# First convolution's weights and patches loaded in two parts, GpSimd's first patch sum behind the centring, 9 fewer small products

## The chip, the cores and the metric

One core of a Trainium2 chip runs the kernel. The metric is the device time of one execution in microseconds (us). The engines are called by the profile's short names: PE is TensorE (PEld its weight loads), DVE is VectorE, ACT is ScalarE, POOL is GpSimd and SP is SyncE, which here only starts DMA transfers. Each engine runs its own instructions in the order in which they stand, and engines wait for each other through semaphores.

## The reference

A batch of 64 images (3 x 84 x 84) goes through a patch embedding, two attentions over patches, two layers of delta attention with a gated feed-forward, and a feed-forward with blockwise quantized operands. The part that the change touches is the first step and what it feeds:

```python
pe = conv_general_dilated(pixel_values, conv_w, (PS, PS), 'VALID')      # PS = 14, C = 256
grid = pe.reshape(b, C, h, CS, h, CS)
red = grid.mean(axis=(3, 5)).reshape(b, C, hw).transpose(0, 2, 1)
win = grid.transpose(0, 2, 4, 3, 5, 1).reshape(b, hw, N, C)
q = _ln(red, la_ln_q_g, la_ln_q_b) @ la_wq
kv = _ln(win, la_ln_kv_g, la_ln_kv_b) @ la_wkv
```

A patch has 3 x 14 x 14 = 588 numbers, so the convolution is a product of a 588 x 256 weight with the patches. Each layer norm subtracts the mean over the 256 channels.

## The kernel before, in words

The 588 input numbers of a patch are padded to five chunks (KC = 5) of 128 partitions. `cw` holds the weights (128 partitions x 5 x 256, f32), `xg` the patches in six groups g of 384 columns each (128 x 5 x 384 per group); both are views of larger tiles, so the profile calls them `cwb` and `big`. There is no scheduler: every engine's order is as written.

- **SP** starts all loads of the beginning back to back on one queue (lines 242 to 253, then 236 and 238): the weights, patch group 0, patch group 1, the vectors, the first part of the token weights `wt`, patch groups 2 and 3, and so on. Each load adds 16 to a semaphore of its own when it has landed.
- **DVE** centres the weights: `centred(at, end, done)` takes the mean over the 256 channels (line 712), divides it by 256 (line 714) and subtracts it (line 716), first for chunks 0 and 1, then for chunks 2 to 4. Each of its three steps adds 1 to the semaphore `cwc`, so that `cwc` is 3 after the first part and 6 after the second. Line 721 then scales the means for a later use, and DVE goes on to sums over the convolution's output (line 726).
- **PE** first multiplies a tile of ones 35 times by itself with 32 x 64 results that nobody reads (`keep_clock_briefly(7, 35)`, line 1428). Then it waits for `cwc` at 3 and for patch group 0, does the products of chunks 0 and 1 for both halves of the channels (line 1436), waits for `cwc` at 6, and does chunks 2 to 4 of group 0 (`conv(0, 0)` and `conv(0, 1)`, line 1265). Products for the vectors, group 1, more weight products and groups 2 to 5 follow. In the profile each f32 product counts twice, so the 35 products are 70 entries and the four of line 1436 are 8.
- **POOL** sets up the ones (line 272) and then sums the three column blocks of each patch group (`patch_sum(g)`, line 289), groups 0 to 2 first, 8 additions in all. The sums of squares `square_sum` (line 296) come behind them on POOL; PE needs the first three in `stat(0)` (line 1297) and the patch sums themselves in `red_mean(0)` (line 1346).
- **ACT** copies the finished convolution chunks out of PSUM (line 345) and squares them (line 338).

Two pairs of semaphores are of interest. `kqb_mm` is raised once after the products of line 1452 and `vb_mm` once after those of line 1457; likewise `gvb_mm` after line 1486 and `ub_mm` after line 1491.

Of the kernel before, what the change touches and what calls it, by code (L numbers as in the profile page):

```python
# [23 lines left out]
KC, KP = 5, 128  # L24
# [36 lines left out]
def build(nc, xp, cw_d, vec_d, wt_d, wl_d, wf_d, cst_d, out):  # L61
    ctx = ExitStack()
    with ctx:
# [17 lines left out]
        ones = sb("ones", [P, P])  # L81
# [4 lines left out]
        part = sb("part", [P, 2, CH, P])  # L86
        redc = sb("redc", [P, CH, NW])
# [117 lines left out]
        def lw(at, n=C, c=CH):  # L205
# [5 lines left out]
        wd = lw(L_D, C, FC)  # L211


        once = """sqsum cw vecs consts tokw tokw2 ffnw cwc ones conv copied squared xsum part redc redq var_mm rsr
            vec_mm vmean cls_v cls_mm kqb_mm kqb vb_mm vbias wkvg wqg q_mm q k_mm1 k_free stat_mm rk softmax score
            attn v_mm1 vprod vsum acc gath aggT mean_mm redb wcen proj_mm loc gq_mm u gvb_mm gvw ub_mm ub sel sql gst_mm
            gsc_mm gv_mm rsg gsm ga_e attp gpr gag_mm gag gp_mm mod_mm xc x_sq x_var x_rs hx m0_mm m0 h0 wq wq_t wqT
            zeros fin_sq fin_ms fin_rs fin_y h1_t h1 stats rs3 xn xq xq_t xqT gu_mm gate hh hq hq_t hqT
            out_mm outs stored"""
# [19 lines left out]

        @blk_.sync  # L240
        def _(sp):
            sp.dma_start(cw[:, :, :], cw_d).then_inc(S["cw"], 16)
            sp.dma_start(xg[:, 0], xp[0]).then_inc(s_x[0], 16)
            sp.dma_start(xg[:, 1], xp[1]).then_inc(s_x[1], 16)
            sp.dma_start(vec[:, :], vec_d).then_inc(S["vecs"], 16)
            sp.dma_start(wt[:, 0:T_PR], wt_d[:, 0:T_PR]).then_inc(S["tokw"], 16)
            sp.dma_start(xg[:, 2], xp[2]).then_inc(s_x[2], 16)
            sp.dma_start(xg[:, 3], xp[3]).then_inc(s_x[3], 16)
            sp.dma_start(wf[:, :], wf_d).then_inc(S["ffnw"], 16)
            sp.dma_start(xg[:, 4], xp[4]).then_inc(s_x[4], 16)  # L250
            sp.dma_start(xg[:, 5], xp[5]).then_inc(s_x[5], 16)
            sp.dma_start(wt[:, T_PR:NTW], wt_d[:, T_PR:NTW]).then_inc(S["tokw2"], 16)
            sp.dma_start(cst[:, :], cst_d).then_inc(S["consts"], 16)
            load_layer(sp, 0, 0)
            load_layer(sp, 0, 1)
            for l in range(1, LAYERS):
                sp.wait_ge(S["wo_mm"], EACH["wo_mm"] * (l - 1) + 2)
                load_layer(sp, l, 0)
                sp.wait_ge(S["dn_mm"], EACH["dn_mm"] * (l - 1) + 2)
                load_layer(sp, l, 1)  # L260

            o_v = out.rearrange("t s c -> s t c")
            for p in range(3):
                sp.wait_ge(S["outs"], p + 1)
                for a in range(2 if p < 2 else 1):
                    sp.dma_start(o_v[2 * p + a], h1[64 * a:64 * a + 64, p, :]).then_inc(S["stored"], 16)
            sp.wait_ge(S["stored"], 16 * SLOTS)


        @blk_.gpsimd  # L270
        def _(pool):
            nc.gpsimd.memset(ones[:, :], 1.0 / C).then_inc(S["ones"], 1)
            nc.gpsimd.memset(h1[:, 2, :], 0.0).then_inc(S["zeros"], 1)

            n = [0]

            def patch_sum(g):

                pool.wait_ge(s_x[g], 16)
                hf = g // 3  # L280
                for a in range(3):
                    new = xg[:, g, :, a * P:(a + 1) * P]
                    first = g % 3 == 0 and a == 1
                    if g % 3 == 0 and a == 0:
                        continue
                    old = xg[:, g, :, 0:P] if first else xs[:, hf]
                    if not first:
                        pool.wait_ge(S["xsum"], n[0])
                    nc.gpsimd.tensor_tensor(xs[:, hf], old, new, ALU.add).then_inc(S["xsum"], 1)  # L289
                    n[0] += 1  # L290

            def square_sum(g):

                pool.wait_ge(S["squared"], 2 * g + 2)
                cols = slice(g % 3 * GRP, (g % 3 + 1) * GRP)
                nc.gpsimd.tensor_tensor(sq[:, 0, cols], sq[:, 0, cols], sq[:, 1, cols], ALU.add  # L296
                                        ).then_inc(S["sqsum"], 1)

            def value_sum(un):

                hf, uu = divmod(un, 5)
                pool.wait_ge(S["vsum"], un + 1)
                old = vsum[:, (un - 1) % 3, :] if uu == 1 else vtot[:, hf, :]
                if uu > 1:
                    pool.wait_ge(S["acc"], 4 * hf + uu)
                nc.gpsimd.tensor_tensor(vtot[:, hf, :], old, vsum[:, un % 3, :], ALU.add
                                        ).then_inc(S["acc"], 2 if uu == 1 else 1)

            for g in range(3):
                patch_sum(g)  # L310
            for g in range(6):
                square_sum(g)
            for un in range(1, 4):
                value_sum(un)
            for g in range(3, 6):
                patch_sum(g)
            for un in range(6, 9):
                value_sum(un)

            pool.wait_ge(S["gag_mm"], 1)  # L320
            nc.gpsimd.memset(act[0:64, FC - 1, :], 0.0).then_inc(S["zeros"], 1)
# [309 lines left out]
        def _(dve):  # L631
# [85 lines left out]
                                ALU.subtract).then_inc(S["cwc"], 1)  # L717

            centred(0, 2, 0)
            centred(2, KC, 3)  # L720
            v.tensor_scalar(cmean9[:, :], cmean[:, :], 1.0 / NP_, None, ALU.mult).then_inc(S["cwc"], 1)

# [132 lines left out]
                step(v.tensor_tensor(clsv[:, 12:13], vmean[:, 0:1], vmean[:, 2:3], ALU.add))  # L855

            def key_weights():
                dve.wait_ge(S["kqb_mm"], 1)
                dve.wait_ge(S["vb_mm"], 1)
                v.tensor_copy(vbias[:, 0:CH], ps[:, 4, 10:12]).then_inc(S["vbias"], 1)  # L860
                for c in range(CH):
                    v.tensor_scalar(wkv[:, c, :], wkv[:, c, :], vec[:, V_LKG + c:V_LKG + c + 1], None, ALU.mult
# [23 lines left out]
            def class_values():  # L886
                dve.wait_ge(S["gvb_mm"], 1)
                for c in range(CH):
                    v.tensor_scalar(gwkv[:, c, C:2 * C], gwkv[:, c, C:2 * C], vec[:, V_GKG + c:V_GKG + c + 1], None,
                                    ALU.mult).then_inc(S["gvw"], 1)  # L890
                dve.wait_ge(S["ub_mm"], 1)
                v.tensor_copy(ub[:, :], ps[:, 6, 0:H]).then_inc(S["ub"], 1)

            for c in range(CH):
# [354 lines left out]
        def _(pe):  # L1249
# [178 lines left out]
                    mm(ps[0:32, bank, 0:64], ones[:, 0:32], ones[:, 0:64], start=True, stop=True)  # L1428

            pe.wait_ge(S["ones"], 1)  # L1430
            keep_clock_briefly(7, 35)
            pe.wait_ge(S["cwc"], 3)
            pe.wait_ge(s_x[0], 16)
            for c in range(CH):
                for k in range(2):
                    mm(ps[:, c, 0:GRP], cwc[:, k, c * P:(c + 1) * P], xg[:, 0, k, :], start=(k == 0), stop=False)
            pe.wait_ge(S["cwc"], 6)
            conv(0, 0)
            conv(0, 1)
            pe.wait_ge(S["ones"], 1)  # L1440
# [14 lines left out]
            for j in range(CH):  # L1455
                for c in range(CH):
                    last = mm(ps[:, 4, 10 + j:11 + j], wkv[:, c, C + j * P:C + (j + 1) * P],
                              vec[:, V_LKB + c:V_LKB + c + 1], start=(c == 0), stop=(c == CH - 1))
            last.then_inc(S["vb_mm"], 1)
            conv(2, 0)  # L1460
            conv(2, 1)
            conv(3, 0)
# [27 lines left out]
            for c in range(CH):  # L1490
                last = mm(ps[:, 6, 0:H], vec[:, V_GKB + c:V_GKB + c + 1].broadcast_to([P, P]), u[:, c, :],
                          start=(c == 0), stop=(c == CH - 1))
            last.then_inc(S["ub_mm"], 1)
            conv(5, 0)
            keys(4)
            conv(5, 1)
# [464 lines left out]
```

## Time and profile before

| | us |
|---|---|
| median of 3 runs | 296.84 |
| lowest and highest of the 3 runs | 293.67 and 297.17 |
| span of the profiled execution, first to last instruction | 292.3 |
| the profiled execution's own device time | not recorded beside the three runs |
| PE busy (products), share of the span | 268.0, 92% |
| DVE busy | 206.8, 71% |
| ACT busy | 94.1, 32% |
| POOL busy | 38.0, 13% |

The span is that of one execution and lies 1.4 us below the lowest of the three runs and 4.5 us below their median. Busy shares are averages over a program with very different parts: in the first 85 us PE is nearly always at work, in the delta attention (about 120 to 150 us and 190 to 220 us) PE and DVE take turns on small tiles, and the last 30 us are led by DVE.

### The profile page before, as it was taken

How to read it: one execution, taken by the hardware profiler on the slowest of the kernel's cores; microseconds unless marked ns; L12 is line 12 of the kernel's file. 1: busy time of each engine (PE TensorE's matmuls, PEld its weight loads, DVE VectorE, ACT ScalarE, POOL GpSimd, SP SyncE). 2: the span in 40 equal slices, each digit the busy share in tenths (PEclk: the TensorE clock that was granted, in tenths of full speed). 3: DMA queues.
4: the chain of work that ended last, by engine and by line, in shares of the span. 5: the costliest groups of instructions: out<-in, count | busy, mean ns of one | idle time of the engine just before them, and what ended most of it. 6: DMA issues, size and time to landing. Idle time of an engine off the chain costs nothing.

```text
span 292.3 us, 9910 instructions
## 1 busy us (share of the span) xinstructions
PE 268.0 (92%) x4473; PEld 205.7 (70%) x4473; DVE 206.8 (71%) x413; ACT 94.1 (32%) x235; POOL 38.0 (13%) x35
## 2 busy tenths in 40 slices
PE   8999999999999899968979999978898999789865
PEld 8666678778997778857857766758876676655443
DVE  3649869987689676467686579675667665498992
ACT  1122301330000026656224432665424343351310
POOL 1991100203893100000000000000000000000000
PEclk9999999999999999999966999997985999999999
DMA  7999900000000000000000302500000000000001
GB/s 287 419 422 419 440 32 0 0 0 2 0 0 2 0 1 3 2 4 0 2 4 13 135 0 75 231 4 2 1 4 2 0 2 0 0 1 2 0 0 45
DMA packets 2730, 18.71 MB, mean 64 GB/s; under 512 B 464, under 2 KB 784, under 8 KB 1936
## 3 DMA queue, kind: packets, MB, share of 16 engines
q1 hardware_dynamic: 2704, 18.34, 15.8%
q8 instruction: 20, 0.33, 0.4%
q14 instruction: 6, 0.05, 0.1%
HBM read 18.01 MB, written 0.33 MB: 63 GB/s over the span
## 4 chain that ended last, share of the span: by engine, by line
PE 74%; DVE 18%; ACT 3%; issue 2%; DMA 2%; SPq 0%; DVEq 0%
PE ps L1265 13%; PE ps L1587 8%; PE ps L1309 5%; PE ps L1799 4%; PE ps L1323 4%; PE ps L1568 3%; PE ps L1688 3%; PE ps L1697 3%; PE ps L1719 2%; DMA big<-in_patches 2%; DVE big L1112 2%; DVE wt L1109 2%; PE ps L1255 2%; PE ps L1771 2%; PE ps L1841 2%
## 5 line engine op out<-in xcount | busy, mean ns | idle before, releaser
L1265 PE MATMUL ps<-big,cwb 128*128 128x384 f32 x112 | 37.9, 489 | 0.0
L1265 PEld LDWEIGHTS ps<-big,cwb 128*128 128x128 f32 x112 | 20.9, 190 | 13.0 <-DVE cwb L716 0.3
L1587 PE MATMUL ps<-xT,wl 128*128 128x320 f32 x88 | 24.5, 434 | 0.7 <-ACT wguT L369 0.5
L289 POOL TENSOR_TENSOR xs<-xs,big 128x640 f32<-128x640 f32 x14 | 23.3, 1667 | 1.4
L1587 PEld LDWEIGHTS ps<-xT,wl 128*128 128x128 f32 x88 | 16.6, 190 | 7.8 <-ACT wguT L369 0.7
L1688 PE MATMUL ps<-wt,big 32*32 32x32 f32 x1280 | 14.8, 199 | 5.7 <-DVE wt L1066 2.8
L345 ACT COPY pecT<-ps 128x384 f32<-128x384 f32 x12 | 5.8, 480 | 40.8 <-PE ps L1265 40.8
L1688 PEld LDWEIGHTS ps<-wt,big 32*32 32x32 f32 x1280 | 13.1, 110 | 8.0 <-DVE big L1112 4.0
L1323 PE MATMUL ps<-wt,pecT 128*128 128x256 f32 x72 | 16.5, 380 | 0.6 <-DVE big L821 0.6
L1309 PE MATMUL ps<-wt,pecT 128*128 128x256 f32 x72 | 16.9, 381 | 0.0
L1109 DVE COPY_PREDICATED wt<-cst,ps 128x320 f32<-128x320 int32 x16 | 8.0, 498 | 10.9 <-PE ps L1697 10.9
L1323 PEld LDWEIGHTS ps<-wt,pecT 128*128 128x128 f32 x72 | 13.5, 190 | 3.0 <-DVE big L821 1.0
L1309 PEld LDWEIGHTS ps<-wt,pecT 128*128 128x128 f32 x72 | 13.4, 190 | 2.3
L1697 PE MATMUL ps<-wt,big 32*32 32x32 f32 x1280 | 13.3, 196 | 0.7 <-issue 0.7
L1799 PE MATMUL ps<-big,wl 128*128 128x320 f32 x48 | 13.3, 434 | 0.0
L1697 PEld LDWEIGHTS ps<-wt,big 32*32 32x32 f32 x1280 | 12.5, 106 | 0.9 <-issue 0.9
L726 DVE TENSOR_REDUCE part<-pecT 128x128 f32<-128x384 f32 x12 | 7.1, 594 | 8.4 <-ACT pecT L345 8.3
L1170 DVE TENSOR_TENSOR cwb<-ps,cwb 128x320 f32<-128x320 f32 (+1 forms) x12 | 5.9, 490 | 9.9 <-PE ps L1587 5.7
L1799 PEld LDWEIGHTS ps<-big,wl 128*128 128x128 f32 x48 | 8.8, 190 | 4.2 <-DVE big L1162 1.0
L499 ACT COPY wt<-ps 128x320 f32<-128x320 f32 x16 | 6.8, 426 | 14.4 <-PE ps L1688 14.4
L296 POOL TENSOR_TENSOR sq<-sq 128x384 f32<-128x384 f32 x6 | 6.2, 1044 | 39.9 <-ACT sq L338 39.9
L1841 PE MATMUL ps<-wguT,pecT 128*128 128x352 f32 x32 | 10.0, 466 | 0.9 <-ACT pecT L592 0.9
(306 smaller groups left out, 535.8 us busy)
## 6 DMA issues: line engine op xcount, KB each, us to landing
big<-in_patches SPq DMA_DIRECT2D x6, 960.0 KB, 11.8
wl<-in_layers SPq DMA_DIRECT2D x2, 2176.0 KB, 19.8
wf<-in_ffn SPq DMA_DIRECT2D x1, 2112.0 KB, 17.9
wl<-in_layers SPq DMA_DIRECT2D x2, 1040.0 KB, 15.9
wt<-in_tok SPq DMA_DIRECT2D x1, 1536.0 KB, 24.8
wt<-in_tok SPq DMA_DIRECT2D x1, 768.0 KB, 8.5
cwb<-in_conv SPq DMA_DIRECT2D x1, 640.0 KB, 3.9
cst<-in_constants SPq DMA_DIRECT2D x1, 320.0 KB, 25.0
```

The source lines that it names most:

```text
L289: nc.gpsimd.tensor_tensor(xs[:, hf], old, new, ALU.add).then_inc(S["xsum"], 1)
L726: step(v.tensor_reduce(part[:, min(g % 3, 1), c, :], pecT[:, c, g * GRP:(g + 1) * GRP].rearrange("p (t n) -> p n t", t=3), AX.X, ALU.add))
L1109: v.copy_predicated(tc_[:, g, :], m.unsqueeze(1).broadcast_to([P, NB, 32]), bank32(6 + b, slice(0, P))).then_inc(S["tp"], 1)
L1265: last = mm(ps[:, i % 4, 0:GRP], cwc[:, k, c * P:(c + 1) * P], xg[:, g, k, :], start=(k == 0), stop=(k == KC - 1))
L1309: last = mm(ps[:, 4 + un % 2, t * C:(t + 1) * C], pecT[:, c, i * P:(i + 1) * P], wkv[:, c, 0:C], start=(c == 0), stop=(c == CH - 1))
L1323: last = mm(ps[:, un % 3, t * C:(t + 1) * C], pecT[:, c, i * P:(i + 1) * P], wkv[:, c, C:2 * C], start=(c == 0), stop=(c == CH - 1))
L1568: last = mm(ps[:, bank, cols], lw(at)[:, c, j * P:(j + 1) * P], src[:, c, cols], start=(c == 0), stop=(c == CH - 1))
L1587: last = mm(ps[:, bank, 0:NT], w(c, j), x[:, c, :], start=(c == 0), stop=(c == CH - 1))
L1688: last = mm(ps[r, 4 + b, 32 * k:32 * k + 32], apm[r, NB * b + k, own], tc_[r, NB * b + k, :], start=True, stop=True)
L1697: last = mm(ps[r, 6 + b, 32 * k:32 * k + 32], ttc[r, NB * b + k, :], yc[r, NB * b + k, :], start=True, stop=True)
L1799: last = mm(ps[:, 6 + j, 0:NT], wd[:, i, j * P:(j + 1) * P], act[:, i, :], start=(i == 0), stop=(i == FC - 1))
L1841: last = mm(ps[:, b + w, 0:352], xqT[:, c, P * p:P * p + P], wguT[:, c, 352 * w:352 * w + 352], start=(c == 0), stop=(c == CH - 1))
```

## The change

On SP the load of the weights becomes two, chunks 0 and 1 and chunks 2 to 4, and so does that of patch group 0; the four go out in the order weights 0-1, patches 0-1, weights 2-4, patches 2-4. Two semaphores, `cw_rest` and `x0_rest`, stand for the second parts: DVE waits for `cw_rest` before the second part of the centring, PE for `x0_rest` before `conv(0, 0)`. POOL's first patch sum waits for `x0_rest` and for `cwc` at 6 as well. The small products of ones on PE are 26 instead of 35. The semaphores `vb_mm` and `ub_mm` are gone: the same instructions raise `kqb_mm` and `gvb_mm` a second time, and the waits ask for 2.

```diff
-            sp.dma_start(cw[:, :, :], cw_d).then_inc(S["cw"], 16)
-            sp.dma_start(xg[:, 0], xp[0]).then_inc(s_x[0], 16)
+            sp.dma_start(cw[:, 0:2, :], cw_d[:, 0:2, :]).then_inc(S["cw"], 16)
+            sp.dma_start(xg[:, 0, 0:2, :], xp[0, :, 0:2, :]).then_inc(s_x[0], 16)
+            sp.dma_start(cw[:, 2:KC, :], cw_d[:, 2:KC, :]).then_inc(S["cw_rest"], 16)
+            sp.dma_start(xg[:, 0, 2:KC, :], xp[0, :, 2:KC, :]).then_inc(S["x0_rest"], 16)
             sp.dma_start(xg[:, 1], xp[1]).then_inc(s_x[1], 16)
@@
                 pool.wait_ge(s_x[g], 16)
+                if g == 0:
+                    pool.wait_ge(S["x0_rest"], 16)
+                    pool.wait_ge(S["cwc"], 6)
@@
             centred(0, 2, 0)
+            dve.wait_ge(S["cw_rest"], 16)
             centred(2, KC, 3)
@@
             def key_weights():
-                dve.wait_ge(S["kqb_mm"], 1)
-                dve.wait_ge(S["vb_mm"], 1)
+                dve.wait_ge(S["kqb_mm"], 2)
@@
-                dve.wait_ge(S["ub_mm"], 1)
+                dve.wait_ge(S["gvb_mm"], 2)
@@
             pe.wait_ge(S["ones"], 1)
-            keep_clock_briefly(7, 35)
+            keep_clock_briefly(7, 26)
             pe.wait_ge(S["cwc"], 3)
             pe.wait_ge(s_x[0], 16)
             ...
             pe.wait_ge(S["cwc"], 6)
+            pe.wait_ge(S["x0_rest"], 16)
             conv(0, 0)
             conv(0, 1)
@@
-            last.then_inc(S["vb_mm"], 1)
+            last.then_inc(S["kqb_mm"], 1)
@@
-            last.then_inc(S["ub_mm"], 1)
+            last.then_inc(S["gvb_mm"], 1)
```

SP's queue at the start of the program, before and after; `cwb` is the weights' tile, `big` the patches', and the numbers are partitions by f32 elements:

```order
L242 DMA cwb<-in_conv 128x1280
L243 DMA big<-in_patches 128x1920
L244 DMA big<-in_patches 128x1920
L245 DMA vec<-in_vectors 128x36
L246 DMA wt<-in_tok 128x1536
```

```order
L242 DMA cwb<-in_conv 128x512
L243 DMA big<-in_patches 128x768
L244 DMA cwb<-in_conv 128x768
L245 DMA big<-in_patches 128x1152
L246 DMA big<-in_patches 128x1920
```

Patch group 1, third in the queue before, is fifth now, and the bytes ahead of it are the same.

PE at the start of the program, before and after; each row names the tile written and the tiles read, the shape, and the semaphores that it waits for:

```order
L1428 MATMUL ps<-ones 32x64 [waits s_ones]
L1428 MATMUL ps<-ones 32x64 x34
L1436 MATMUL ps<-big,cwb 128x384 [waits s_patches0,s_cwc]
L1436 MATMUL ps<-big,cwb 128x384 x3
L1265 MATMUL ps<-big,cwb 128x384 [waits s_patches0,s_cwc]
L1265 MATMUL ps<-big,cwb 128x384 x5
```

```order
L1433 MATMUL ps<-ones 32x64 [waits s_ones]
L1433 MATMUL ps<-ones 32x64 x25
L1441 MATMUL ps<-big,cwb 128x384 [waits s_patches0,s_cwc]
L1441 MATMUL ps<-big,cwb 128x384 x3
L1270 MATMUL ps<-big,cwb 128x384 [waits s_patches0,s_x0_rest,s_cwc]
L1270 MATMUL ps<-big,cwb 128x384 x5
```

Nothing changes place on PE; nine small products are gone, and the row of chunks 2 to 4 waits for one thing more.

## Rows read from the trace of the kernel before

**Rows 1.** the page: the span, and the chain that ended last by engine

```profile
span 292.3 us, 9910 instructions
...
PE 74%; DVE 18%; ACT 3%; issue 2%; DMA 2%; SPq 0%; DVEq 0%
```

**Rows 2.** the chain that ended last: start us, us, what

```profile
7.14 2.82 PE ps L1436 x8
...
14.16 3.33 PE ps L1265 x10
...
45.54 1.90 PE ps L1297 x18
...
82.84 1.85 PE ps L1309 x8
84.78 0.70 DVE prod L763
```

**Rows 3.** windows, PE alone: window, us, PE busy (x entries), granted clock, DMA share, GB/s

```profile
10.00:40.00 30.00, 30.00 (x115) 1.00 0.92 384
40.00:84.50 44.50, 44.50 (x229) 1.00 0.00 1
```

**Rows 4.** timeline of PE: start us, us, instruction, [idle before <-releaser]

```profile
0.99 5.89 PE L1428 MATMUL ps<-ones 128*32 128x64 f32 x70 [0.99 <-POOL ones L272]
7.14 2.82 PE L1436 MATMUL ps<-big,cwb 128*128 128x384 f32 x8 [0.25 <-DMA big<-in_patches]
```

**Rows 5.** timeline of SP: when each DMA is issued, and for how long

```profile
0.74 0.38 SPq L242 DMA_DIRECT2D cwb<-in_conv  x1
1.18 0.42 SPq L243 DMA_DIRECT2D big<-in_patches  x1
1.64 0.43 SPq L244 DMA_DIRECT2D big<-in_patches  x1
```

**Rows 6.** issue to landing, lines 242, 243 and 244 in this order

```profile
DMA to landing us min/median/max: 3.9/3.9/3.9
...
DMA to landing us min/median/max: 5.8/5.8/5.8
...
DMA to landing us min/median/max: 7.8/7.8/7.8
```

**Rows 7.** DMA issues by line: KB each, median us from issue to landing

```profile
out<-h SPq DMA_DIRECT2D x5, 64.0 KB, 2.0
```

**Rows 8.** timeline of DVE: the centring of the weights

```profile
4.68 0.69 DVE L712 TENSOR_REDUCE cmean<-cwb 128x2 f32<-128x512 f32 x1 [4.68 <-DMA cwb<-in_conv]
5.40 0.17 DVE L714 TENSOR_SCALAR cmean<-cmean 128x2 f32<-128x2 f32 x1
5.61 0.69 DVE L716 TENSOR_TENSOR cwb<-cwb,cmean 128x512 f32<-128x512 f32 x1
6.21 0.95 DVE L712 TENSOR_REDUCE cmean<-cwb 128x3 f32<-128x768 f32 x1
7.20 1.44 DVE L714 TENSOR_SCALAR cmean<-cmean 128x3 f32<-128x3 f32 x1
8.67 0.96 DVE L716 TENSOR_TENSOR cwb<-cwb,cmean 128x768 f32<-128x768 f32 x1
```

**Rows 9.** windows, PE alone, over the small products of ones

```profile
0.98:4.78 3.80, 3.79 (x36) 1.00 0.77 274
4.78:6.72 1.94, 1.94 (x37) 1.00 1.01 420
```

**Rows 10.** timeline of POOL: the 8 patch sums of groups 0 to 2

```profile
7.07 1.54 POOL L289 TENSOR_TENSOR xs<-big 128x640 f32<-128x640 f32 x1 [5.88 <-DMA big<-in_patches]
8.69 12.16 POOL L289 TENSOR_TENSOR xs<-xs,big 128x640 f32<-128x640 f32 x7
```

**Rows 11.** windows, PE alone, two later stretches

```profile
148.20:158.30 10.10, 8.76 (x136) 0.50 0.01 2
...
216.50:226.60 10.10, 8.64 (x174) 0.50 0.01 3
```

More of the change, by code:

```diff
@@ L211, in build @@
         wd = lw(L_D, C, FC)
-        once = """sqsum cw vecs consts tokw tokw2 ffnw cwc ones conv copied squared xsum part redc redq var_mm rsr
-            vec_mm vmean cls_v cls_mm kqb_mm kqb vb_mm vbias wkvg wqg q_mm q k_mm1 k_free stat_mm rk softmax score
-            attn v_mm1 vprod vsum acc gath aggT mean_mm redb wcen proj_mm loc gq_mm u gvb_mm gvw ub_mm ub sel sql gst_mm
+        once = """sqsum cw cw_rest x0_rest vecs consts tokw tokw2 ffnw cwc ones conv copied squared xsum part redc redq var_mm rsr
+            vec_mm vmean cls_v cls_mm kqb_mm kqb vbias wkvg wqg q_mm q k_mm1 k_free stat_mm rk softmax score
+            attn v_mm1 vprod vsum acc gath aggT mean_mm redb wcen proj_mm loc gq_mm u gvb_mm gvw ub sel sql gst_mm
             gsc_mm gv_mm rsg gsm ga_e attp gpr gag_mm gag gp_mm mod_mm xc x_sq x_var x_rs hx m0_mm m0 h0 wq wq_t wqT
```

## Prediction

> **What bounds the kernel now.** I read the page first: the span of the profiled execution is 292.3 us, and 74% of the chain that ended last is PE [rows 1]. The chain itself tells where a change at the start of the program counts. It runs through PE from 7.14 us, when the first real product starts, to 84.8 us, where DVE takes over [rows 2], and the windows show PE busy in all of 10 to 84.5 us [rows 3]. So for the first 85 us PE works down its list without a pause. An earlier start of that list moves everything up to there by as much, if no load and no other engine gets in the way. Behind 84.8 us each step waits for the one before it, so the lead should be kept to the end.
>
> What sets the start at 7.14 us? On PE the small products of ones begin at 0.99 us and are through at some 6.8 us; then PE is idle 0.25 us for patch group 0 [rows 4]. Group 0 is issued at 1.18 us [rows 5] and lands 5.8 us later [rows 6], at 6.98 us. The centring of chunks 0 and 1 on DVE is through at 5.61 + 0.69 = 6.30 us [rows 8]. So three things meet before the first product: ones, centring, patches, and the patches are last.
>
> **The loads.** Weights land at 0.74 + 3.9 = 4.64 us, group 0 at 6.98, group 1 at 1.64 + 7.8 = 9.44 [rows 5, 6]. A group is 128 x 1920 x 4 bytes = 960 KB, and two of them took 2.34 and 2.46 us, so the queue moves some 410 KB per us. The 640 KB of weights then account for 1.56 us of the time before 4.64, and 3.08 us is where the stream effectively starts. In the new order 256 KB of weights land at 3.08 + 0.62 = 3.70 us, 384 KB of patches at 4.64, 384 KB of weights at 5.58, and the last 576 KB at 6.98. SP needs 0.44 to 0.46 us from one issue to the next [rows 5], so the fourth load goes out at about 2.1 us and group 1 at about 2.5 instead of 1.64. It was in flight for 7.8 us, nearly all of it queueing, so 0.9 us of later issue does not move its landing at 9.44. PE reaches it at 14.16 us before [rows 2] and would at 12.7 now, 3.3 us after the landing. The loads behind it go out 0.9 us later too, and are covered in the same way.
>
> The split is the unknown of this change: no row shows a 256 KB load at the head of the queue. The bounds are from below the stores of 64 KB, 2.0 us from issue to landing [rows 7], which with the 192 KB more at 410 KB per us give 0.74 + 2.0 + 0.47 = 3.2 us; and from above the landing of the whole weights, 4.64 us. I take 3.70, by the two landings of the same queue.
>
> The Trainium skill, page "DMA: Bandwidth & Descriptors", section "Anatomy of one DMA", gives a load a fixed cost of about 2.0 us and its bytes at 436 GB/s on top; by that, an estimate from the page, the first weights would land at 0.74 + 2.0 + 0.6 = 3.3 us. That lies near my lower bound, and as the next parts show it would change nothing, since another term comes last.
>
> **The centring.** The first part takes from 4.68 to 6.30 us, 1.62 us [rows 8]. From 3.74 it ends at 5.36 us. The second part has no wait before; now it waits for weights 2-4 at 5.58 us. It took from 6.21 to 9.63 us, 3.42 us, of which the small step of line 714 is 1.44, against 0.17 for its twin on chunks 0 and 1 [rows 8]. That step runs from 7.20 to 8.64 us, and POOL's first patch sum from 7.07 to 8.61 [rows 10]: DVE's step ends as POOL's does, 0.03 us later. With POOL's sum behind `cwc` at 6 the 1.27 us go. The second part then takes 2.15 us, from 5.62 to 7.77. If the stall had another cause and stayed, it would end at 9.04.
>
> **The small products.** They set the start now. The first 36 entries take 3.79 us, 105 ns each, the other 34 take 1.94 us, 57 ns each [rows 9]. The granted clock reads 1.00 in both windows, but the pace nearly doubles, so PE went from the lower of its two levels (1.2 GHz) to the higher (2.4 GHz) at about 4.78 us, after 3.8 us of unbroken small products. 26 products are 52 entries: 36 until 4.78 us, and 16 x 57 ns = 0.91 us, which ends at 5.69. The centring (5.36) and patches 0-1 (4.64) are ready before. The first real product starts at about 5.7 us instead of 7.14, which is a gain of **1.4 us**. PE goes over from the ones to the real products without a pause, where it paused for 0.25 us before, so I expect no fall of the clock.
>
> Here the Trainium skill has a rule against the change: page "TensorE: Matmul & The Clock Gate", Part 1, says that the rise of the clock is bought with a time of sustained work and not with a number of products, and comes at another moment in every run. It is the clock rival below.
>
> **Chunks 2 to 4.** The 8 entries of line 1436 take 2.82 us [rows 4], so PE asks for the rest at 5.7 + 2.8 = 8.5 us. The second centring is there at 7.77, 0.7 us ahead, and patches 2-4 at 6.98, 1.5 us ahead: the new wait on PE costs nothing. Were the stall on DVE still there, PE would wait about 0.5 us. Before, this step was ready at 9.63 and PE at 9.96, so it is no gain by itself: POOL's delay only keeps the earlier start from being lost here.
>
> **What is delayed.** POOL's 8 patch sums now start at about 7.8 us instead of 7.07. They take until 8.69 + 12.16 = 20.85 us [rows 10] and would end at about 21.6. Queued behind them are the sums of squares, for which PE waits at 45.5 us [rows 2], 44.1 when moved up: over 20 us of cover. POOL's overlap moves from line 714 to the step of line 721 and to DVE's later small steps, which it slowed before as well; DVE's first sum of the convolution waits for ACT anyway. Price 0, at most some tenths on DVE that PE, which alone is on the chain there [rows 2], does not feel.
>
> **The semaphores.** The merged pairs are raised by the same PE instructions in the same order, and each reader waits for the value that the later one gives. Price 0; one wait fewer on DVE.
>
> **Sum.** 292.3 - 1.4 = 290.9 us of span. The profiled span lies 4.5 us below the median of the three runs, and I take that distance as it is: 296.84 - 1.4 = **295.4 us**, 0.5% faster.
>
> **Rivals.**
>
> 1. *The first part doesn't land earlier (the split doesn't do what it says).* If weights 0-1 land at 4.64 us, the centring ends at 6.3 and PE starts at 6.35: gain 0.8 us, 296.0. Landings between give between 0.8 and 1.4. For it: no row has a short load at the head of the queue. Against it: the queue has a steady pace over three loads. If the four shorter loads also slow the stream, it is about even, 296.8.
>
> 2. *A half-speed stretch of PE falls elsewhere.* The profile has two stretches of 10 us at a granted clock of 0.50 (the 1.2 GHz level), 148.2 to 158.3 and 216.5 to 226.6, with PE busy for 8.76 and 8.64 us in them [rows 11]. Work bound by PE takes twice as long there, so one is worth up to 4.4 us, and as part of it is waiting I put it at 3. They begin in or behind the small-tile work of the attention, which moves by 1.4 us. One fewer gives about 292.4, one more 298.4. The three runs before, 3.5 us apart, look like just that. It happens with and without the change, so it widens the range more than it moves the time.
>
> 3. *The clock rises late, and the kernel gets slower.* The place is PE between 5.7 and 10 us. With 52 entries all at the low level the ones end at 0.99 + 52 x 0.105 = 6.45 us, and the real products then run at half pace until the clock rises. The cost against the forecast is 0.75 us for the later end and half of the time from 6.45 to the rise. It turns into a loss when the rise comes later than about 7.8 us, against 4.78 in the profile; a rise at 10 us gives 0.75 + 1.8 = 2.55, so 298.0 us. For it: fewer ones are left as a reserve. Against it: the real products follow at once and keep PE busy, and a late rise made the 70 entries of before later too.
>
> 4. *The gain is lost at another wait within the first 85 us.* That needs an engine or load that lags PE by less than 1.4 us now. The chain shows only PE there, so I give it little: 296.8.
>
> **How the numbers follow.** Forecast (1.0 to 1.6 us gained): 0.60, 295.4. Rival 1: 0.13, 296.0 to 296.8. Rival 2: one stretch fewer 0.08, 292.4; one more 0.09, 298.4. Rival 3: 0.04, 298.0. Rival 4: 0.06, 296.8. The median of three runs of before is itself one draw from 293.7 to 297.2, which enters each case. The range 292.2 to 298.2 holds the forecast with rivals 1, 3 and 4 and about half of each side of rival 2. Faster by over 2% would be below 290.9 us, slower by over 2% above 302.8; 2% is about what a measurement of this kernel can tell from no change. No case reaches either; I leave 0.03 and 0.01.
>
> **What would show it.** In the profile after: the first load lands at about 3.7 us after the span's start, DVE's first reduction starts then and line 719 (714 before) takes 0.17 us both times; the small products end at about 5.7 and the first real product follows at once; POOL starts at about 7.8; `conv(0, 0)` has no wait; each later product of PE up to 83 us starts 1.4 us earlier. I am wrong if the first real product starts after 6.4 us, if PE waits before chunks 2 to 4, or if the lead seen at 10 us is gone by 85.

## The result and the profile after

The changed kernel takes 298.05 us (median of 14 runs, 295.12 to 299.53), the kernel before 296.63 (median of 14, 293.67 to 298.77). The ratio is 1.0078, with a 95% interval of 1.0049 to 1.0107: slower by 0.8%, where I had forecast 0.5% faster. All ratios here leave out executions over 1.5% above the fastest of their kernel, here three of the kernel before (298.19 to 298.77) and none of the changed one; over all executions the means are 1.5 us, 0.5%, apart. The profiled execution has a span of 296.9 us, 4.6 more than that of before [rows 1]:

```profile
span 296.9 us, 9876 instructions
...
PE 76%; DVE 16%; issue 3%; ACT 2%; DMA 2%; SPq 0%; DVEq 0%
```

In the chain that ended last, "issue" (the engine waits for nothing that the profile shows) has gone from 2% to 3%, and PE from 74% to 76%.

**The start.** PE's timeline of the changed kernel (start, us, instruction, idle before) answers to [rows 4]:

```profile
0.99 5.40 PE L1433 MATMUL ps<-ones 128*32 128x64 f32 x52 [0.99 <-POOL ones L274]
6.33 2.85 PE L1441 MATMUL ps<-big,cwb 128*128 128x384 f32 x8
9.53 4.14 PE L1270 MATMUL ps<-big,cwb 128*128 128x384 f32 x12 [0.36 <-DVE cwb L721]
...
33.30 0.60 PE L1281 MATMUL ps<-ones,redq 128*128 128x1 f32 x4
```

The first real product starts at 6.33 us instead of 7.14, the products of chunks 2 to 4 at 9.53, where the timeline of the kernel before has:

```profile
9.79 4.03 PE L1265 MATMUL ps<-big,cwb 128*128 128x384 f32 x12
```

In the changed kernel they waited for DVE's centring. DVE's timeline, against [rows 8]:

```profile
3.58 0.69 DVE L717 TENSOR_REDUCE cmean<-cwb 128x2 f32<-128x512 f32 x1 [3.58 <-DMA cwb<-in_conv]
...
7.33 0.95 DVE L717 TENSOR_REDUCE cmean<-cwb 128x3 f32<-128x768 f32 x1 [2.14 <-DMA cwb<-in_conv]
8.32 0.17 DVE L719 TENSOR_SCALAR cmean<-cmean 128x3 f32<-128x3 f32 x1
8.52 0.96 DVE L721 TENSOR_TENSOR cwb<-cwb,cmean 128x768 f32<-128x768 f32 x1
...
31.67 1.12 DVE L742 SCALAR_TENSOR_TENSOR redc<-part 128x256 f32<-128x256 f32 x1
```

The stall of line 714 is gone: 0.17 us at 8.32, where it was 1.44. But the second centring starts at 7.33 us, because it waited for weights 2-4. From issue to landing, lines 242 to 245 (weights 0-1, patches 0-1, weights 2-4, patches 2-4), against [rows 6]:

```profile
DMA to landing us min/median/max: 2.8/2.8/2.8
...
DMA to landing us min/median/max: 3.4/3.4/3.4
...
DMA to landing us min/median/max: 5.7/5.7/5.7
...
DMA to landing us min/median/max: 6.6/6.6/6.6
```

Issued at 0.74, 1.18, 1.64 and 2.12 us, the four land at 3.5, 4.6, 7.3 and 8.7. The first two come as forecast (3.70, 4.64), the other two 1.7 us later than forecast (5.58, 6.98).

The last rows of the two timelines show where even the small lead ends. DVE's `redc` step, 0.42 us before, takes 1.12 us at 31.67, while a sum of squares of POOL runs from 31.51 to 32.50 us. ACT's square and PE's line 1281 come behind it, and PE is then 0.1 us behind the old kernel instead of 0.15 ahead.

**The loops.** So the start is even, and the 4.6 us come later. The list of PE's waits without a visible cause (line, total, times, longest), before:

```profile
PE ps L1697 <- issue: 0.7, 2, 0.4
...
PE ps L1712 <- issue: 0.5, 2, 0.2
...
PE ps L1734 <- issue: 0.2, 1, 0.2
```

and after:

```profile
PE ps L1703 <- issue: 3.7, 2, 2.3
...
PE ps L1740 <- issue: 1.2, 2, 1.0
...
PE ps L1718 <- issue: 0.5, 2, 0.2
```

That is 1.4 us before and 5.4 after. They lie in and just behind the two loops over small 32 x 32 products (lines 1688 and 1697 of before, in a hardware loop of four rounds with 320 entries and as many weight loads each, once in each attention layer). PE's timeline there, before:

```profile
125.83 0.89 PE L1688 MATMUL ps<-wt,big 32*32 32x32 f32 x80
128.11 0.89 PE L1688 MATMUL ps<-wt,big 32*32 32x32 f32 x80 [1.40 <-DVE wt L1066]
128.85 0.58 PE L1697 MATMUL ps<-wt,big 32*32 32x32 f32 x45
129.72 1.20 PE L1697 MATMUL ps<-wt,big 32*32 32x32 f32 x115 [0.29 <-issue]
...
142.32 1.31 PE L1712 MATMUL ps<-pecT,cst 128*128 128x320 f32 x4 [0.24 <-issue]
...
198.79 1.59 PE L1697 MATMUL ps<-wt,big 32*32 32x32 f32 x124 [0.40 <-issue]
```

and after:

```profile
126.94 0.89 PE L1694 MATMUL ps<-wt,big 32*32 32x32 f32 x80
128.43 0.89 PE L1694 MATMUL ps<-wt,big 32*32 32x32 f32 x80 [0.59 <-DVE wt L1071]
129.16 0.73 PE L1703 MATMUL ps<-wt,big 32*32 32x32 f32 x63
132.23 1.54 PE L1703 MATMUL ps<-wt,big 32*32 32x32 f32 x97 [2.34 <-issue]
...
145.19 1.31 PE L1718 MATMUL ps<-pecT,cst 128*128 128x320 f32 x4 [0.24 <-issue]
...
150.25 0.25 PE L1740 MATMUL ps<-wt,big 32*32 32x32 f32 x4 [1.01 <-issue]
...
202.67 1.12 PE L1703 MATMUL ps<-wt,big 32*32 32x32 f32 x106 [1.32 <-issue]
```

In the old kernel the first half of a round is 80 entries, then 80 that wait for DVE (1.40 us), then come 45 of the 160 entries of the second half; PE pauses 0.29 us and goes on. In the new one PE comes 63 entries far and pauses 2.34 us. 63 is 45 + 18, and 18 entries are the 9 small products that were taken out at the start of the program. The pause stands at a fixed distance in the instruction stream from the start, not at a fixed place in the code.

The longer pauses, 4.0 us more in sum, do not simply add up to 4.0 of the 4.6 us. PE is 0.26 us ahead of the old kernel at 122 us, 1.1 behind at the start of the first loop (126.94 against 125.83), 2.9 behind after it (line 1718 against 1712), 3.7 at the start of the second loop, 3.2 after that one and 4.6 at the end. The 1.4 us between 122 and the first loop fall in a stretch in which the granted clock reads 0.51, where the old kernel's reads 1.00:

```profile
121.90:125.30 3.40, 3.40 (x70) 0.51 0.02 5
```

Of the lateness at the first loop 0.8 us are made good, since the wait for DVE is shorter by that much (0.59 instead of 1.40 us); the pause of 2.34 us comes on top. So this one profile mixes two things, the pauses and the clock; run b26 below shows the first of them without a difference ahead of the loop.

What PE seems to wait for is in the transfers of the instruction queue, which the page gives as 20 packets of 0.33 MB in both kernels, 16 KB each. One of them starts in 127.4 to 128.1 us before and none between 126.0 and 127.4:

```profile
q8 instruction: 1, 0.02, 8.6%
```

In the changed kernel there is none from 126.0 to 129.4 us; it starts after that, in 129.4 to 131 us:

```profile
q8 instruction: 1, 0.02, 5.4%
```

By the trace's transfer records the starts are 127.48 and 129.47 us. PE's pause ends 2.2 us after the first (129.72) and 2.8 after the second (132.23). In the old kernel the block was under way while PE waited for DVE anyway; in the new one its transfer started only 1.0 us behind that wait, in the middle of dense products. In all 17 profiles this pause ends 2.2 to 2.8 us after such a transfer starts; that PE waits for its own instructions is read from this and from the place that moves with them.

The Trainium skill, page "Runtime: NRT & Kernel Launch", section "Instruction fetch mechanics", describes this as PE's instruction memory being refilled in blocks of 16 KiB by the sequencer's own queue, mostly hidden, except that a taken branch to a target outside the two blocks at hand forces a fetch first. The 16 KB agree with the trace's packets; that the cost is mostly hidden holds here only for some placements.

### The profile page after: what moved, and what is told of

Read it like the earlier page. It is cut to its first block, busy times and chain, and to the rows that moved or that the text cites. A ratio compares the mean times of both kernels' runs of the same rounds, so it can differ in the third digit from the quotient of the medians.

```text
span 296.9 us, 9876 instructions
## 1 busy us (share of the span) xinstructions
PE 270.7 (91%) x4455; PEld 206.9 (70%) x4455; DVE 205.4 (69%) x413; ACT 94.0 (32%) x235; POOL 37.1 (13%) x35
## 4 chain that ended last, share of the span: by engine, by line
PE 76%; DVE 16%; issue 3%; ACT 2%; DMA 2%; SPq 0%; DVEq 0%
PE ps L1270 12%; PE ps L1593 8%; PE ps L1314 5%; PE ps L1805 4%; PE ps L1328 4%; PE ps L1847 3%; PE ps L1574 3%; PE ps L1694 3%; PE ps L1703 3%; PE ps L1428 3%; DVE big L1117 2%; DMA cwb<-in_conv 2%; DVE wt L1114 2%; PE ps L1260 2%; PE ps L1771 2%
## 5 line engine op out<-in xcount | busy, mean ns | idle before, releaser
L294 POOL TENSOR_TENSOR xs<-xs,big 128x640 f32<-128x640 f32 x14 | 22.5, 1610 | 1.4
```

## The experiments

Two theories stood at first. P: the number of PE instructions ahead of the loops decides where an instruction block ends in them, and the 9 products taken out moved it badly. L: the split loads cost the time. All ratios are to the kernel before, and "pauses" is the sum of PE's waits on "issue" in the run's profile, as above.

### One part at a time

```diff
 # a35: the changed kernel
-            keep_clock_briefly(7, 26)
+            keep_clock_briefly(7, 35)
 # b26: the kernel before
-            keep_clock_briefly(7, 35)
+            keep_clock_briefly(7, 26)
 # split35: as a35
-                    pool.wait_ge(S["cwc"], 6)
 # pool35: the kernel before
                 pool.wait_ge(s_x[g], 16)
+                if g == 0:
+                    pool.wait_ge(S["cwc"], 6)
```

> The changed kernel with 35 small products instead of 26. Theory P (placement of PE's instructions): the loss comes from PE's pauses without a visible cause in the two loops of small-tile products (5.4 us in the profile of the changed kernel, 1.4 us in that of before), and these depend on how many PE instructions stand ahead of the loops; with 35 they fall back to under 2.5 us and the ratio to before is 0.997 to 1.003. Theory L (the split loads cost the time): weights 2-4 still land at about 7.3 us, and the ratio stays at 1.005 to 1.010.

> The kernel before with 26 small products and nothing else changed. Theory P: PE's unexplained pauses rise to 4 to 6 us and the ratio to before is 1.005 to 1.011, though the first real product starts at 7.1 us as before. Theory L: nothing that matters is changed, ratio 0.998 to 1.002.

> The changed kernel with 35 small products and POOL's first patch sum waiting only for its patches. Theory P: ratio 0.997 to 1.003, unexplained pauses under 2.5 us. Theory L: 1.005 to 1.012. POOL starts at about 8.7 us, when patches 2-4 land, and slows the centring of weights 2-4 by up to 1.3 us, so the first conv(0) product of chunks 2 to 4 starts later than in the changed kernel's 9.5 us.

> The kernel before with only POOL's first patch sum behind the centring (cwc at 6). Theory P: ratio 0.998 to 1.003; line 714's second execution takes 0.17 us instead of 1.44, the centring is through at 8.4 instead of 9.6 us, and PE, which asked at 9.8, gains nothing. Theory L: the same. A third theory, D (POOL's later sums slow DVE's small steps at 22 to 33 us): PE waits about 0.3 us before line 1276 and the ratio is 1.001 to 1.003.

| run | ratio to before, 95% interval | pauses, us |
|---|---|---|
| a35 | 1.0007 (0.9972 to 1.0042) | 2.3 |
| b26 | 1.0104 (1.0050 to 1.0158) | 3.9 |
| split35 | 0.9981 (0.9947 to 1.0015) | 4.0 |
| pool35 | 1.0001 (0.9966 to 1.0037) | 1.3 |

b26 has nothing of the change but the 9 products, whose end PE did not even wait for, and it is 1% slower. a35 has all of the change but those, and is even. That is theory P and against L. PE's timeline of b26, first half of a round and the pauses:

```profile
128.93 0.73 PE L1697 MATMUL ps<-wt,big 32*32 32x32 f32 x63
131.57 1.54 PE L1697 MATMUL ps<-wt,big 32*32 32x32 f32 x97 [1.92 <-issue]
...
145.08 1.31 PE L1712 MATMUL ps<-pecT,cst 128*128 128x320 f32 x4 [0.24 <-issue]
...
202.11 1.65 PE L1697 MATMUL ps<-wt,big 32*32 32x32 f32 x106 [0.75 <-issue]
```

63 entries and a pause of 1.92 us, at the same place as in the changed kernel, with the loads of before. Up to the first loop this profile is a constant 0.07 us behind that of the kernel before; after the loop it is 2.8 us behind (145.08 against 142.32), and 2.6 at the end. Practically the whole loss arises in that one loop.

The pause itself grew by only 1.6 us of these 2.7 (1.92 instead of 0.29). Soon after it begins, from 130.3 us on, the granted clock reads 0.50 for 6.8 us, and in the same window of the kernel before 1.00 (b26 first, then before):

```profile
130.30:137.10 6.80, 5.40 (x385) 0.50 0.01 2
130.30:137.10 6.80, 5.75 (x587) 1.00 0.01 2
```

All seven profiles with 22, 26, 28, 39 or 44 products' worth of instructions ahead of the first loop have such a stretch of 3.4 to 6.9 us somewhere from 130 to 140 us, and so has split35's; the nine others, all with 31, 32 or 35, have none. So the block's place costs time in two ways, by the pause and by a stretch at the lower clock level that comes with it: 1.6 us and, as the difference, an estimated 1.1 us in b26. In all of them the pause begins before the clock falls. No run has one without the other, so how much of a ratio belongs to which stays open.

The 4.0 us of pauses of split35 are from an execution of 298.04 us, its slowest; the other eleven took 293.32 to 296.62 us. The expectation of under 2.5 us was not met in it; the ratio came as expected.

pool35 shows that POOL's delay does remove the stall (line 714 took 0.17 us and the centring was through at 8.4 us) and brings nothing by itself. In its profile the clock rose only at 6.9 us and the first real product started at 7.82, so the earlier centring could not show there. Theory D, that POOL's later sums cost time on PE, was not seen there; it is seen in the profiles of the changed kernel, a35 and afterpad, where POOL starts at 9.3 us or later: `redc` takes 1.12 to 1.13 us in these three and 0.42 to 0.43 in all others, and PE loses 0.25 us at line 1281.

### Elsewhere, and other counts

```diff
 # afterpad: the changed kernel (26 at the start), at about 102 us
             keep_clock(0, 1, 192)
+            for _ in range(9):
+                mm(ps[0:32, 0, 0:8], ones[:, 0:32], ones[:, 0:8], start=True, stop=True)
 # b31, b22, b44: the kernel before
-            keep_clock_briefly(7, 35)
+            keep_clock_briefly(7, 31)   # 22, 44
```

> The changed kernel (26 small products at the start) with 9 tiny products of ones (32 x 8 results that nobody reads) added far later, at about 102 us, where PE waits 0.7 us for DVE anyway. Theory P says that only the number of PE instructions ahead of the loops counts: the pauses without a visible cause fall under 2.5 us and the ratio to before is 0.996 to 1.002. Theory W (the 9 products are missed at the start, as warm-up of the clock): the pauses stay at 4 to 6 us and the ratio at 1.005 to 1.010.

> The kernel before with 31 small products (4 fewer). Theory P: the time is a step or a saw-tooth in the number of instructions, so this lies either with 35 (ratio 0.998 to 1.002, pauses under 2.5 us) or with 26 (1.005 to 1.012, pauses of 3 us or more), not between them. A theory in which each missing product costs its share gives 1.004 to 1.005.

> The kernel before with 22 small products (13 fewer). Theory P: as bad as 26 or back to the level of 35, by its pauses (3 us or more: 1.005 to 1.012; under 2.5 us: 0.998 to 1.002). A theory in which each missing product costs its share gives 1.014.

> The kernel before with 44 small products (9 more). They end at about 7.2 to 7.8 us, so the first real product starts up to 0.6 us later. Theory P: pauses anywhere between 0 and 6 us, and the ratio follows them: 1.000 to 1.003 with pauses under 2.5 us, 1.007 or more with 4 us. A theory in which each product saves its share gives 0.991 to 0.993.

afterpad is the decisive run: it gives back the 9 products' instructions, but not at the start. Ratio 0.9978 (0.9934 to 1.0023), pauses 1.1 us. The pause is back at 45 entries and short:

```profile
129.90 0.58 PE L1705 MATMUL ps<-wt,big 32*32 32x32 f32 x45
130.71 1.20 PE L1705 MATMUL ps<-wt,big 32*32 32x32 f32 x115 [0.23 <-issue]
...
199.73 1.57 PE L1705 MATMUL ps<-wt,big 32*32 32x32 f32 x124 [0.38 <-issue]
```

Theory W (the products are missed as warm-up) expected 1.005 to 1.010 and falls. The counts:

| small products (kernel before) | ratio, 95% interval | pauses, us |
|---|---|---|
| 22 | 1.0176 (1.0111 to 1.0240) | 5.6 |
| 26 | 1.0104 (1.0050 to 1.0158) | 3.9 |
| 28 | 1.0088 (1.0047 to 1.0130) | 3.1 |
| 31 | 0.9974 (0.9926 to 1.0022) | 1.2 |
| 35 | 1 | 1.4 |
| 39 | 1.0084 (1.0040 to 1.0128) | 6.2 |
| 44 | 1.0197 (1.0139 to 1.0256) | 8.7 |

More products than 35 cost as much as fewer than 31. A part of that is the start, which the small products themselves now hold up: chunks 2 to 4 start at 10.76 us with 39 and at 11.45 with 44 instead of 9.79, in profiles in which the clock rose at 6.5 and 6.8 us. The rest goes with the pauses (the 6.2 us of 39 are from an execution of 302.67 us, where the median is 298.16). With 44 the pauses are others: PE stops a second time near the end of the first round, for the next block, and again in the second layer:

```profile
131.77 1.30 PE L1697 MATMUL ps<-wt,big 32*32 32x32 f32 x128 [0.85 <-issue]
135.77 0.25 PE L1697 MATMUL ps<-wt,big 32*32 32x32 f32 x5 [2.70 <-issue]
...
206.10 1.30 PE L1697 MATMUL ps<-wt,big 32*32 32x32 f32 x128 [2.04 <-issue]
209.55 0.43 PE L1697 MATMUL ps<-wt,big 32*32 32x32 f32 x14 [2.15 <-issue]
```

Between its two pauses in the first round stand 128 entries and as many weight loads, 256 instructions. If one 16 KB transfer brings just these, an instruction has 64 bytes; the 9 products taken out, 18 entries and 18 weight loads, are then 2.3 KB of a block.

In b22 about 1.7 us of the loss is something else. The 22 products end 2.01 us before the first real product starts, which waits for the patches, and 0.4 us after that start the granted clock falls from 1.00 to 0.50 (the 1.2 GHz level) for 3.4 us (window, us, PE busy, granted clock):

```profile
5.30:7.20 1.90, 0.09 (x1) 1.00 1.05 428
7.50:10.90 3.40, 3.40 (x7) 0.50 1.01 406
10.90:14.00 3.10, 3.10 (x10) 1.00 1.02 426
```

The 8 entries of chunks 0 and 1 take 4.51 us there instead of 2.82. In b26's profile the gap was 1.70 us and the clock stayed at 1.00 until 130 us, where the pause is, so b26's loss is not this.

### Between the loops

```diff
 # b26mid: as b26, and in layer 1, ahead of its loop
-                    keep_clock(0, 2, 512)
+                    keep_clock(0, 1, 512)
+                    for _ in range(10):
+                        mm(ps[0:32, 0, 0:8], ones[:, 0:32], ones[:, 0:8], start=True, stop=True)
```

> The kernel before with 26 small products at the start and, between the two loops of small-tile products (at about 181 us, in place of one 512-column filler product), 10 tiny products of ones, so that the second loop has as many PE instructions ahead of it as in the kernel before and the first has 36 fewer. Theory P (placement): around the first loop the pauses are those of 26 products (1.3 to 2.5 us, and 0.3 to 1.0 us some 18 us later), around the second those of before (0.2 to 0.9 us); ratio between the two, 1.003 to 1.008. A theory in which something at the start of the program slows both loops keeps both, ratio 1.008 to 1.012.

Ratio 1.0113 (1.0047 to 1.0179), above the 1.003 to 1.008 that I expected for the total. The places of the pauses came as expected:

```profile
132.62 1.54 PE L1699 MATMUL ps<-wt,big 32*32 32x32 f32 x97 [2.11 <-issue]
...
151.22 0.25 PE L1736 MATMUL ps<-wt,big 32*32 32x32 f32 x4 [0.93 <-issue]
...
203.43 1.79 PE L1699 MATMUL ps<-wt,big 32*32 32x32 f32 x124 [0.52 <-issue]
```

Around the first loop they are those of b26 (97 entries left behind the pause, 2.11 us, and 0.93 us later); in the second layer the pause lies at the place of before (124 entries left) and takes 0.52 us, with none in line 1736. Since b26's own second loop cost only 0.75 + 0.22 us in its profile, only some 0.5 us was there to be saved, too little for the intervals to show. That the total did not fall stays unexplained; in its profile the clock is at the lower level from 121.7 to 125.1 and from 132.0 to 138.8 us, in b26's only in the second place.

### The loads

```diff
 # split31: as split35
-            keep_clock_briefly(7, 35)
+            keep_clock_briefly(7, 31)
 # wfirst31: the changed kernel, 31 products (line not shown)
             sp.dma_start(cw[:, 0:2, :], cw_d[:, 0:2, :]).then_inc(S["cw"], 16)
+            sp.dma_start(cw[:, 2:KC, :], cw_d[:, 2:KC, :]).then_inc(S["cw_rest"], 16)
             sp.dma_start(xg[:, 0, 0:2, :], xp[0, :, 0:2, :]).then_inc(s_x[0], 16)
-            sp.dma_start(cw[:, 2:KC, :], cw_d[:, 2:KC, :]).then_inc(S["cw_rest"], 16)
 # xsplit31: the changed kernel, 31 products (line not shown), weights whole
-            sp.dma_start(cw[:, 0:2, :], cw_d[:, 0:2, :]).then_inc(S["cw"], 16)
+            sp.dma_start(cw[:, :, :], cw_d).then_inc(S["cw"], 16)
             sp.dma_start(xg[:, 0, 0:2, :], xp[0, :, 0:2, :]).then_inc(s_x[0], 16)
-            sp.dma_start(cw[:, 2:KC, :], cw_d[:, 2:KC, :]).then_inc(S["cw_rest"], 16)
@@
-            dve.wait_ge(S["cw_rest"], 16)
```

> The changed loads with 31 small products and POOL's first sum waiting for its patches alone. Theory P: pauses under 2.5 us. The start: ones end at 6.2 to 6.5 us, weights 2-4 land at 6.5 to 7.7 us as in the three runs that had these loads, so the products of chunks 2 to 4 start at 9.0 to 9.9 us against 9.79 before; ratio 0.994 to 1.000. If the load order cost nothing (my forecast's 5.58 us for weights 2-4), they would start at 8.9 us.

> As the changed kernel with 31 small products, and the second part of the weights issued ahead of the first part of the patches. If shorter loads as such slow the stream (theory S), patches 0-1 land at 6 to 7 us instead of 5.6 and the first real product starts at 6.3 to 7.0; weights 2-4 land at 4.7 to 5.5 us and the second centring is through by 7.8. If only the place in the queue matters, weights 2-4 land at 4.6 us and patches 0-1 at 5.6. Chunks 2 to 4 start at 9.0 to 9.6 us, ratio 0.993 to 0.999.

> As the changed kernel with 31 small products, but the weights loaded whole and only patch group 0 in two parts. Weights land at 4.7 us, centring of chunks 0 and 1 through at 6.3, patches 0-1 at 5.6 to 6.2: first real product at 6.4 us, second centring through at 8.5 without POOL's stall, chunks 2 to 4 at 9.1 us against 9.79 before. Theory S: patches 2-4 land at 7.5 to 8.5 us instead of 7.0, which still costs nothing. Ratio 0.993 to 0.999.

| run | landings in the order of issue, us | chunks 2 to 4 start, us | ratio |
|---|---|---|---|
| changed kernel | 3.5, 4.6, 7.3, 8.7 | 9.53 | 1.0078 (1.0049 to 1.0107) |
| split31 | 3.5, 4.5, 6.6, 8.1 | 8.96 | 0.9974 (0.9938 to 1.0011) |
| wfirst31 | 3.5, 4.6, 6.1, 8.7 | 9.07 | 0.9977 (0.9935 to 1.0018) |
| xsplit31 | 4.6, 5.7, 7.2 | 9.78 | 0.9992 (0.9953 to 1.0031) |

These loads have the same bytes in all versions, and before the last of them landed at 6.98 us. In three parts it lands 0.2 us later, in four 1.1 to 1.7 us in this table and 2.1 in a35. Patch group 1 behind them lands at 9.7 us (xsplit31), 10.5 (split31) and 11.1 to 11.2 (wfirst31, the changed kernel) instead of 9.44. So the place of one load in the queue is not what costs: in both orders of four the last lands late. Theory S puts it down to the number of short loads. xsplit31 fits that, but it also leaves the weights whole, so whether the number counts or the cut in the weights' load is not shown. In xsplit31 the weights were in time, but the clock rose only at 6.3 us, the 31 small products ended at about 7.0, and the first real product started at 7.09. For wfirst31 the second centring is through at 7.2 us, so its chunks 2 to 4 follow without a wait:

```profile
6.38 2.85 PE L1441 MATMUL ps<-big,cwb 128*128 128x384 f32 x8
9.07 4.03 PE L1270 MATMUL ps<-big,cwb 128*128 128x384 f32 x12
```

That is the forecast mechanism at work: 9.07 instead of 9.79 us, 0.7 us of lead. split31 has 0.8 us of lead at 81 us and 1.2 us at 110, and then loses all of it in one stretch (0.2 us behind at 126 us):

```profile
120.60:124.00 3.40, 3.40 (x83) 0.51 0.02 5
```

With the granted clock at 0.51 (nearly all of it at the 1.2 GHz level), the 80 entries of line 1664 take 2.37 us instead of 1.56 and those of line 1677 1.83 instead of 1.13. In the old kernel the same work ran at 1.00. The wait for DVE in the loop is then shorter here, so the second 80 products start 0.3 us ahead again. The two profiles differ in where the clock falls, and the profiles of wfirst31, split35, b26mid and the changed kernel have a fall between 120 and 122 us too. Whether an earlier start makes that fall likelier is not settled by one profile each.

### The steps, and the forecast start on its own

> The kernel before with 28 small products (28 fewer PE instruction entries than with 35). The time was level at 31 and 35 and some 1% up at 26. Theory P with one step where an instruction block's border passes a wait: either level (0.995 to 1.002, pauses under 2.5 us) or up (1.005 to 1.012, pauses over 3 us). A gradual loss would give 1.003 to 1.006.

> The kernel before with 39 small products (16 more entries than with 35). 44 gave 1.020. Level (0.996 to 1.003, a little later start by 0.2 us) if the second step lies between 39 and 44, or up by 1% or more with pauses over 4 us if it lies below 39.

b28 is at 1.0088 and b39 at 1.0084 (table above). Both are up, so the level stretch is narrow: 31 and 35 in, 28 and 39 out. By these ratios it is a step between 28 and 31 and not a slope: the intervals of 28 and 31 do not meet. The pause says the same (1.87 us in the first loop with 28, 0.47 with 31). The ratio of 28 alone would be weak evidence: the means over all executions, 297.68 us for b28 and 297.02 for the kernel before, are only 0.7 us apart.

> All weights ahead of the patches as in the run of that order with 31, but 26 small products at the start and 6 tiny ones at 102 us, so that 32 products' worth of instructions stand ahead of the loops. Weights 2-4 land at 5 us, patches 0-1 at 6.2, the first real product starts at 6.2 us or, if the clock rises late, when the ones end; chunks 2 to 4 at 8.9 us without a wait. Theory P: pauses under 2.5 us. Ratio to before 0.993 to 0.999. If the lead is lost again at a half-speed stretch of PE's clock around 120 us, 0.997 to 1.000.

Edit: wfirst31 with 26 small products at the start and 6 of the tiny ones at 102 us. Ratio 0.9994 (0.9944 to 1.0045), pauses 2.7 us, a little over the 2.5 that theory P allowed. The patches landed at 6.84 us, so the first real product started at 6.93 us and chunks 2 to 4 at 9.58: no earlier than with 31. No version is shown to be faster than the kernel before: the best four (b31, split31, wfirst31, afterpad) lie at 0.9974 to 0.9978, each with an interval that reaches over 1.

## Why the prediction was wrong

The measured 298.05 us lie inside my range of 292.2 to 298.2, but that is luck: the range was wide for other reasons, and none of its cases has instruction blocks in it.

- **"The first real product starts at about 5.7 us" (small products).** It was 6.33. The clock rose at 5.9 us in this execution and not at 4.78, so 46 entries of the small products ran at the slow pace. This is my rival 3 in a small size, worth 0.6 us. I had taken the moment of one execution for a property of the kernel; over the 17 profiles the rise comes at 4.0 to 6.9 us. The rule of the Trainium skill that I cited there (page "TensorE: Matmul & The Clock Gate", Part 1), that a count of products does not buy the rise, agrees with this.
- **The loads.** First part right (3.5 and 4.6 us). Weights 2-4 at 7.3 instead of 5.58: the pace of 410 KB per us, read from long loads, does not hold for four shorter ones in the first 9 us. Rival 1 had this in its last sentence ("If the four shorter loads also slow the stream, it is about even, 296.8"), at a small chance; a35, with the same loads and all 35 products, is even (1.0007). That PE would ask at 8.5 us and find the second centring done since 7.77 failed by this (it was done at 9.48), and the start's gain shrank from 1.4 to 0.26 us. The estimate from the Trainium skill's page "DMA: Bandwidth & Descriptors" (section "Anatomy of one DMA"), 3.3 us for the first landing, was 0.2 us short of the 3.5; the page gives its figures for transfers issued by GpSimd, and these are SP's.
- **The stall of line 714.** Right in cause and size: it is gone in all runs where POOL waits for the centring, and present (1.39 to 1.43 us) in b22, b26, b26mid, b28, b31, b39 and b44, where nothing about POOL is changed. pool35, with that one edit, shows the cause. In split35 and split31 POOL waits for patches 2-4 alone and starts late enough; the small step behind the centring takes 1.5 us there, as in the kernel before.
- **What is delayed ("Price 0").** Nearly. POOL started at 9.66 us and not at 7.8, its patch sums ended at 22.6, and its third sum of squares ran beside DVE's `redc`; PE lost 0.25 us there.
- **"Nothing changes place on PE; nine small products are gone": the step that failed.** So says the section on the change, and the prediction follows it: I priced the products by their own time, and the sum has no term for what their absence does to the rest of PE's list; I put it at nothing without a reason. The instructions do not change order, but all that follow stand 36 instructions (18 entries and 18 weight loads) earlier in the stream, and in the first loop the pause is 2.34 us instead of 0.29. Cost alone: b26, 1.0104; taken back: a35, 1.0007, and afterpad, 0.9978. The 1.4 us of "issue" was in the trace of before, in the list of PE's waits, and I passed over it as small.
- **Rival 2 (another half-speed stretch).** It came too: the profile of the changed kernel has the clock at the lower level for some 31 us between its start and 290 us, that of the kernel before for some 24. I took such stretches for chance, equal with and without the change. The one from 132.2 to 135.6 us is one of those that come with the long pause. The mean granted clock of the 14 executions is 0.937 to 0.954, and no execution with 22, 26 or 28 products' worth of instructions ahead of the loops (44 with these 14) is above that; of the 97 of the kernel before that ran beside the experiments, 53 read 0.957 or more.
- **"The lead should be kept to the end".** Not testable on the changed kernel, which had none. In split31 the 0.8 us of lead at 9 us were 1.2 at 110 and 0.3 at 128.

The wrong sign comes from the step that failed, since a35 and afterpad, which differ from the changed kernel only in these instructions, are even; the first two points explain why no gain stood against it.

## What to carry to other kernels

Taking out or adding instructions ahead of a dense stretch or a loop can move where its instruction blocks end, and here that was worth 1%. Before calling such an edit free, look for PE waits on "issue", and compare with a variant that has the same number of instructions and puts the fillers where the engine waits anyway (as afterpad did); a difference of 1% between two counts is no verdict on what the instructions do.

When a load is cut in parts, cost the case that the later parts land late (here by 1.7 us) and leave slack for the wait behind them. And take the moment of the clock's rise from several executions, not from one.

## What the runs showed of the hardware

- The pause in the first loop stood at 27, 37, 45, 53, 59, 63 and 71 of 160 entries for 44, 39, 35, 31, 28, 26 and 22 small products, two entries per product, and at the same place in every variant with that number of products ahead of the loop, wherever they stood (51 for the 32 of wfirstpad).
- It ended 2.2 to 2.8 us after the start of a 16 KB transfer on the instruction queue. With 31 to 44 products that transfer started while PE waited for DVE between the first two groups of 80 entries, or just as that wait ended; with 22 to 28 it started only 1.0 to 1.4 us after the end of the wait. Why it isn't asked for earlier stays open; placing the loop itself on a block's border wasn't tried.
- In eight profiles (the changed kernel, b22, b26, b26mid, b28, b39, b44 and split35) the granted clock read 0.50 or 0.51 for 3.4 to 6.9 us in or behind the pauses of the first loop, which are 1.09 to 2.70 us at their longest there. In the nine others, with 0.23 to 1.15 us, it read 1.00 from 128 to 142 us.
- A gap of 2.01 us between the small products and the first real one was followed by a stretch at a granted clock of 0.50 in b22, from 0.4 us after the gap; gaps of 1.70, 1.32 and 0.89 us (b26, b28, b26mid) were not.
